# First experts of a two-layer transformer block: the neighbouring chunks' steps spread over a chunk's sixteen steps

## The chip, the cores and the metric

The kernel runs on one core of one Trainium2 chip. The metric is the device time of one execution in microseconds. Five engines work in parallel, each with its own instruction list: PE (TensorE, matmuls), DVE (VectorE), ACT (ScalarE), POOL (GpSimd) and SP (SyncE, which here issues all DMAs). They meet only through semaphores.

## What is computed

The input is 4 sequences of 1024 tokens with 128 features, fp32. Two layers follow each other, each attention and then a mixture of experts, with a layer norm after each half:

```python
x = _layernorm(x + _L0_attn_ref(x, Wqkv, Wout))        # 16 heads, causal, scores clipped
x = _layernorm(x + _L0_ffn_ref(x, Wg, W1, W2, W3))     # 8 experts, top 2, silu(x W1) * (x W2), then W3
x = _layernorm(x + _L1_attn_ref(x, w_qkv, w_out, b))   # 16 heads, full, rotary turn of q and k
x = _layernorm(x + _L1_ffn_ref(x, ...))                # 4 experts, top 2, gelu
```

Both expert layers compute all experts for all tokens and weigh them by gates, which are zero for the experts not chosen. The change lies in the second line, the first experts.

## The kernel before

Tokens go through the first experts in eight chunks of 512, features on the partitions. A chunk has sixteen steps (`SPC`), one for each tile of 128 hidden features, two steps for each of the eight experts. In a step n of chunk c:

- PE (`pe_chunk`) first runs what `pe_beside` has for the step, then the six hidden matmuls of step n + 3 (three for W1, three for W2, since each fp32 operand is split into an upper and a lower part), then the three matmuls of the product with W3.
- ACT (`act_chunk`) takes silu of the first hidden bank and copies the upper part of the previous step's product (`act_upper`), then runs `act_beside` for step n - 2.
- DVE (`dve_chunk`) multiplies the two hidden halves (L1447), subtracts to get the lower part of the step before (L1436), runs `dve_beside` for step n - 2, and in even steps weighs one expert's output by its gates (`dve_weigh`, L1427). Weighing 0 writes `y_sb`, the others write a part that POOL adds to it.
- POOL (`pool_experts0`) has one fixed list for a chunk: seven adds of weighed outputs (`pool_add`), the `pow` of both layer norms, and small pieces for the neighbours.

ACT and DVE are two steps late against PE (`LATE`); in the last steps of a chunk they reach into the next one's loop.

The "beside" steps belong to the neighbouring chunks. The front is chunk c + 1, which is still being prepared: output projection of the attention (`o_proj`), residual and statistics, normalisation (`norm`), turn into features by tokens (`x_turn`), router matmuls (`router`), the best two (`dve_top2`), the gates' weights (`weigh`), their turn (`g_turn`), from where SP stores and broadcasts them. The back is chunk c - 1, whose experts are done: turn of its output (`y_turn`), residual and statistics, normalisation into `x_out` (`norm2`), its turn (`x2_turn`), and the next layer's queries (`q`), keys (`k`) and values (`v`). Queries and keys get their rotary turn on DVE (L1370, L1371), are summed on POOL (`pool_rot`), copied by ACT, and their lower parts come from POOL (`pool_qk_lower`). `plan[0]` (L993) says in which of the sixteen steps each of these happens; all engines read the same table. Chunk 0 has no back, chunk 7 has no front, and after chunk 7 its own back steps run alone, between them the first score pairs of the next attention (`BESIDE_BACK`, L131).

Waits that matter here: `x_turn` on PE waits for DVE's normalisation; ACT at `norm2` copies `x_out` and at `x_turn` copies the turned tile twice, in program order; the router's matmuls wait for both of these copies; `x2_turn` waits for `norm2` and for `gate_pre`, the last instruction of the top two, as they share a PSUM bank; `v` waits for the keys' rotation; weighing 0 waits for `y_turn` of the chunk before. The reciprocals of the softmax sums (`dve_rcp`, L1378) run at beside-step 7, written as a number.

Of the kernel before, what the change touches and what calls it, by code (L numbers as in the profile page):

```python
# [15 lines left out]
B, T, D, H = 4, 1024, 128, 16  # L16
# [108 lines left out]
class Full:  # L125
# [2 lines left out]
    HEADS = (1, 3, 0, 2)  # L128
    TURN_0, TURN_1 = 10, 2
    FIRST = PAIRS - 2 * PAIRS_STEP  # L130
    BESIDE_BACK = {1: (0,), 2: (1,), 4: (2, 3), 7: (4,), 8: (5, 6), 9: (7,)}  # L131

    def __init__(self, sem):
        self.n = 1
# [72 lines left out]
def build_program(nc, d, out):  # L207
    with ExitStack() as ctx:
# [537 lines left out]
        def first_pairs(L):  # L746

            return range(1 + max(m for ms in L.BESIDE_BACK.values() for m in ms), L.FIRST)

        def pe_pair_beside_back(pe, L, n):  # L750

            for m in L.BESIDE_BACK.get(n, ()):
                if m == 0:
# [237 lines left out]
            pass  # L991

        plan = [Beside(), Beside()]  # L993
        for pl, steps in ((plan[0], (2, 4, 6, 7, 8, 9, 1, 1, 3, 4, None, 5, 8, 10)),
                          (plan[1], (5, 7, None, None, None, None, 1, 1, 3, 6, 8, 11, 13, None))):
            (pl.y_turn, pl.norm2, pl.x2_turn, pl.q, pl.k, pl.v,
             pl.o_turn, pl.o_proj, pl.norm, pl.x_turn, pl.hidden, pl.router, pl.weigh, pl.g_turn) = steps
# [517 lines left out]
        def pool_rstd(pool, pc, wait, sig, k, val):  # L1515
            pool.wait_ge(wait, val)
            pool.sem_inc(apart_pool, 1)
            pc.link(nc.gpsimd.tensor_scalar(rstd[:, k, :], mv[:, k, :, 1], EPS, None, ALU.add))
            nc.gpsimd.tensor_tensor(rstd[:, k, :], rstd[:, k, :], mhalf[:, :], ALU.pow).then_inc(sig, 1)
# [45 lines left out]
        def pool_experts0(pool, st):  # L1565
# [3 lines left out]
            for c in range(2 * B + 1):  # L1569
# [9 lines left out]
                    pool_fill_values(pool, layers[1])  # L1579
                if c > 0:  # L1580
                    pool_rstd(pool, pc, st.stats2, st.rstd2, 1, c)
                if front:
                    pool_x_lower(pool, st, c + 1)
                if c < 2 * B:
                    pool_add(pool, st, c, 1, 0)
                if front:
                    pool_gate_exp0(pool, st, c + 1)
                if c < 2 * B:
                    pool_add(pool, st, c, 2, 0)
                if c > 0:  # L1590
                    for a in range(2):
                        pool_rot(pool, st, c - 1, a)
                if c < 2 * B:
                    pool_add(pool, st, c, 3, 0)
                if c > 0:
                    for a in range(2):
                        pool_qk_lower(pool, st, c - 1, a)
                if c < 2 * B:
                    pool_add(pool, st, c, 4, 0)
                    pool_add(pool, st, c, 5, 0)  # L1600

        def pool_experts1(pool, st):
            pc = Chain(pool, st.pool_chain)
# [248 lines left out]
```

## Time and profile before

| | us |
|---|---|
| median of 3 runs | 1602.66 (1599.79 to 1603.99) |
| profiled execution | 1611.3 |
| its span, first to last instruction | 1609.5 |
| of it, the first experts (chunks 0 to 7) | about 317 to 681 |
| PE busy in the span | 1471.5 (91%) |
| DVE busy | 1400.4 (87%) |
| ACT busy | 1202.9 (75%) |
| POOL busy | 307.5 (19%) |
| mean granted TensorE clock | 0.952 of full |

The times in the profile are those of one execution. "Idle before" is the time that an engine stood still before an instruction, with the instruction that released it behind the arrow. Matmuls are pipelined, so starts are safer to read than durations.

### The profile page before, as it was taken

The page shows a single profiled execution, that of the slowest core. Times are in us where ns is not written, and L with a number is a line of the kernel's source. Part 1 is how long each engine was busy: PE and PEld are TensorE (multiplying, and loading weights), DVE is VectorE, ACT ScalarE, POOL GpSimd, SP SyncE. Part 2 cuts the span into 40 slices and gives each one's busy share as a digit, 9 for nine tenths or more (in the row PEclk, how much of TensorE's full clock was granted, in tenths as well). Part 3 has the DMA queues.
Part 4 walks back from the last instruction along what each step waited for, and adds up shares of the span by engine and source line. Part 5 has one row for each costly group of instructions (what it writes and reads, how often), then busy time and mean ns, then how long its engine had stood idle before and what let it go on. Part 6 is the DMA issues. An engine that isn't in the chain of part 4 may idle for free.

```text
span 1609.5 us, 32282 instructions
## 1 busy us (share of the span) xinstructions
PE 1471.5 (91%) x11200; PEld 797.1 (50%) x11200; DVE 1400.4 (87%) x2394; ACT 1202.9 (75%) x1897; POOL 307.5 (19%) x325
## 2 busy tenths in 40 slices
PE   7989898689999999969999999999999998999996
PEld 4333333377777777623333333333333334777775
DVE  5899999878888988887999999999999973788886
ACT  4999999644445454417999999999999986777775
POOL 0000000234455454420000000000000001234333
PEclk9899999799999998966999999999999997999999
DMA  6636432131224431111111111111111110211211
GB/s 203 203 106 182 120 102 86 49 107 40 96 93 127 128 108 66 66 41 51 46 37 37 46 45 38 42 37 36 37 36 36 37 32 28 69 56 63 75 56 40
DMA packets 71026, 116.76 MB, mean 73 GB/s; under 512 B 23808, under 2 KB 33920, under 8 KB 70272
## 3 DMA queue, kind: packets, MB, share of 16 engines
q1 hardware_dynamic: 70912, 115.21, 23.5%
q8 instruction: 75, 1.23, 0.3%
q14 instruction: 39, 0.32, 0.1%
HBM read 73.49 MB, written 41.16 MB: 71 GB/s over the span
## 4 chain that ended last, share of the span: by engine, by line
PE 61%; DVE 15%; ACT 10%; issue 10%; POOL 1%; DMA 1%; DVEq 0%; ACTq 0%; SPq 0%; POOLq 0%
PE full_o L718 14%; PE hid_pair L1031 12%; PE max_pair L689 11%; ACT cprobs L491 7%; PE bank L1134 7%; DVE negmax_h L808 5%; PE score L703 4%; PE causal_o L463 3%; PE triple L447 2%; PE bank L1066 2%; ACT o_sb L779 1%; DVE st L1284 1%; PE hid_pair L952 1%; PE bank L1094 1%; DVE hid_lo L1458 1%
## 5 line engine op out<-in xcount | busy, mean ns | idle before, releaser
L771 ACT ACTIVATE probs<-score 128x512 f32<-128x512 f32 x1024 | 546.6, 596 | 89.5 <-PE score L703 69.5
L808 DVE TENSOR_REDUCE negmax_h<-max_pair 128x2 f32<-128x1024 f32 x512 | 588.6, 1216 | 24.9 <-PE max_pair L689 24.8
L718 PE MATMUL full_o<-probs,v_st 128*32 128x256 f32 x4096 | 337.9, 403 | 17.7 <-ACT o_sb L779 17.7
L703 PE MATMUL score<-q_st,k_st 32*128 32x512 f32 x1024 | 319.9, 510 | 2.6 <-ACT probs L771 2.6
L689 PE MATMUL max_pair<-k_st,q_st 32*128 32x512 f32 x1024 | 264.7, 515 | 12.2 <-DVE negmax_h L808 10.8
L491 ACT ACTIVATE cprobs<-triple 128x1536 f32<-128x1536 f32 x192 | 258.4, 1713 | 5.2 <-PE triple L447 5.2
L689 PEld LDWEIGHTS max_pair<-k_st,q_st 32*128 32x128 f32 x1024 | 97.8, 188 | 236.7 <-DVE negmax_h L808 179.9
L1240 ACT ACTIVATE act_s<-hid_pair 128x512 f32<-128x512 f32 x128 | 76.7, 599 | 149.5 <-PE hid_pair L1031 149.5
L1031 PE MATMUL hid_pair<-x_hi,w_hi 128*128 128x512 f32 x384 | 171.3, 446 | 1.8 <-DVE x_lo L1401 1.0
L521 DVE TENSOR_SCALAR cprobs<-cprobs 128x1536 f32<-128x1536 f32 (+6 forms) x272 | 160.7, 618 | 2.9 <-ACT cprobs L491 2.9
L463 PE MATMUL causal_o<-cprobs,v_st 128*32 128x512 f32 (+3 forms) x1536 | 156.2, 502 | 2.2 <-DVE cprobs L521 2.2
L718 PEld LDWEIGHTS full_o<-probs,v_st 128*32 128x32 f32 x4096 | 83.3, 109 | 150.0 <-issue 94.5
L703 PEld LDWEIGHTS score<-q_st,k_st 32*128 32x128 f32 x1024 | 141.6, 187 | 28.8 <-ACT probs L771 19.5
L1031 PE MATMUL hid_pair<-x_lo,w_hi 128*128 128x512 f32 x384 | 154.6, 403 | 0.0
L1031 PE MATMUL hid_pair<-x_hi,w_lo 128*128 128x512 f32 x384 | 154.3, 402 | 0.0
L447 PE MATMUL triple<-q_st,k_st 32*128 32x512 f32 (+3 forms) x768 | 101.5, 429 | 28.7 <-ACT cprobs L491 26.0
L447 PEld LDWEIGHTS triple<-q_st,k_st 32*128 32x128 f32 x768 | 47.6, 186 | 135.5 <-ACT cprobs L491 127.1
L1248 ACT ACTIVATE hid_hi<-hid_pair,be 128x512 fp32r<-128x512 f32 x128 | 89.0, 695 | 24.9 <-PE hid_pair L1031 17.9
L1134 PE MATMUL bank<-hid_hi,w_hi 128*128 128x512 f32 x256 | 101.9, 398 | 1.4 <-DVE qk_lo L1436 1.3
L1134 PE MATMUL bank<-hid_hi,w_lo 128*128 128x512 f32 x256 | 101.4, 396 | 0.0
L568 POOL COPY v_st<-v_all 128x256 f32<-128x256 f32 x32 | 12.7, 400 | 434.6 <-PE causal_o L463 246.3
L520 DVE SCALAR_TENSOR_TENSOR cprobs<-cprobs,bound 128x256 f32<-128x256 f32 (+4 forms) x160 | 92.3, 577 | 3.9 <-ACT cprobs L491 2.5
(157 smaller groups left out, 2001.8 us busy)
## 6 DMA issues: line engine op xcount, KB each, us to landing
gate_all<-gate_scr SPq DMA_DIRECT2D x48, 512.0 KB, 4.3
o_scr<-o_sb SPq DMA_DIRECT2D x64, 256.0 KB, 2.1
k_st<-k_scr SPq DMA_DIRECT2D x64, 128.0 KB, 2.8
q_st<-q_scr SPq DMA_DIRECT2D x128, 64.0 KB, 2.5
k_st<-k_scr SPq DMA_DIRECT2D x64, 96.0 KB
q_st<-q_scr SPq DMA_DIRECT2D x64, 96.0 KB
q_scr<-qk_hi SPq DMA_DIRECT2D x18, 256.0 KB, 4.6
k_scr<-qk_hi SPq DMA_DIRECT2D x18, 256.0 KB, 4.5
```

The costliest lines, as they stand in the source:

```text
L447: last = nc.tensor.matmul(triple[n % 2][:, bk, off:off + w], k_st[p][rows, kt * P:(kt + 1) * P], q_st[p][rows, q0:q0 + w], start=True, sto ...
L463: last = nc.tensor.matmul(causal_o[qc][SLOT * j:SLOT * (j + 1), c0:c0 + w], v_st[p][:, kt, j, :], cprobs[at % CP][:, bk, off:off + w], sta ...
L491: nc.scalar.activation(cprobs[n % CP][:, :, :], triple[n % 2][:, :, :], ACT.Exp, scale=SCALE).then_inc(L.exp_done, 1)
L520: nc.vector.scalar_tensor_tensor(edge, edge, float(np.exp(-CLIP)), limit, ALU.max, ALU.min)
L521: ins = nc.vector.tensor_scalar(plain, plain, float(np.exp(-CLIP)), float(np.exp(CLIP)), ALU.max, ALU.min)
L689: last = nc.tensor.matmul(ring[slot][:, k, :], q_st[p][rows, qt * P:(qt + 1) * P], k_st[p][rows, half * CH:(half + 1) * CH], start=True, s ...
L703: nc.tensor.matmul(sbank[L.score_bank(e)][:, :], k_st[p][rows, kt * P:(kt + 1) * P], q_st[p][rows, q0:q0 + w], start=True, stop=True, tile ...
L718: last = nc.tensor.matmul(full_o[SLOT * j:SLOT * (j + 1), cols], v_st[p][:, kt, j, :], probs[s % NP][:, j, cols], start=(kt == 0 and part ...
L771: nc.scalar.activation(probs[s % NP][:, L.HEADS[j], :], sbank[L.score_bank(e)][:, :], ACT.Exp, scale=SCALE).then_inc(L.exp_done, 1)
L808: nc.vector.tensor_reduce(negmax_h[:, qt // TPC, half, heads[0]:heads[1] + 1:2, qt % TPC], ring[slot][:, :, :], AXX, ALU.max, negate=True) ...
L1031: last = nc.tensor.matmul(hbank[2 * k + n % h_banks[layer]], w[:, slice_of(n)], x[:, :], start=(a == 0), stop=(a == 2))
L1134: last = nc.tensor.matmul(y_bank[e % 2], w, x, start=(f == 0 and a == 0), stop=(f == per - 1 and a == 2))
```

## The change

The steps of the table for the first experts are moved: `y_turn` 2 to 3, `norm2` 4 to 6, `x2_turn` 6 to 8, `q` 7 to 9, `k` 8 to 11, `v` 9 to 12, `norm` 3 to 4, `x_turn` 4 to 6, `router` 5 to 7, `weigh` 8 to 10, `g_turn` 10 to 13. The output projection stays at 1. The pairs beside the last back steps are renumbered with them. POOL's list is reordered: each add comes one place earlier, the two rotation sums are separated by an add, and the two lower parts of q and k go to the end of the list.

```diff
-    BESIDE_BACK = {1: (0,), 2: (1,), 4: (2, 3), 7: (4,), 8: (5, 6), 9: (7,)}
+    BESIDE_BACK = {2: (0,), 3: (1,), 6: (2, 3), 9: (4,), 11: (5, 6), 12: (7,)}
...
-        for pl, steps in ((plan[0], (2, 4, 6, 7, 8, 9, 1, 1, 3, 4, None, 5, 8, 10)),
+        for pl, steps in ((plan[0], (3, 6, 8, 9, 11, 12, 1, 1, 4, 6, None, 7, 10, 13)),
                           (plan[1], (5, 7, None, None, None, None, 1, 1, 3, 6, 8, 11, 13, None))):
             (pl.y_turn, pl.norm2, pl.x2_turn, pl.q, pl.k, pl.v,
              pl.o_turn, pl.o_proj, pl.norm, pl.x_turn, pl.hidden, pl.router, pl.weigh, pl.g_turn) = steps
...
                 if c > 0:
                     pool_rstd(pool, pc, st.stats2, st.rstd2, 1, c)
+                if c < 2 * B:
+                    pool_add(pool, st, c, 1, 0)
                 if front:
                     pool_x_lower(pool, st, c + 1)
                 if c < 2 * B:
-                    pool_add(pool, st, c, 1, 0)
+                    pool_add(pool, st, c, 2, 0)
                 if front:
                     pool_gate_exp0(pool, st, c + 1)
                 if c < 2 * B:
-                    pool_add(pool, st, c, 2, 0)
+                    pool_add(pool, st, c, 3, 0)
                 if c > 0:
-                    for a in range(2):
-                        pool_rot(pool, st, c - 1, a)
+                    pool_rot(pool, st, c - 1, 0)
                 if c < 2 * B:
-                    pool_add(pool, st, c, 3, 0)
+                    pool_add(pool, st, c, 4, 0)
+                if c > 0:
+                    pool_rot(pool, st, c - 1, 1)
+                if c < 2 * B:
+                    pool_add(pool, st, c, 5, 0)
                 if c > 0:
                     for a in range(2):
                         pool_qk_lower(pool, st, c - 1, a)
-                if c < 2 * B:
-                    pool_add(pool, st, c, 4, 0)
-                    pool_add(pool, st, c, 5, 0)
```

## Rows read from the trace of the kernel before

**Rows 1.** Table by stretches, chunks from step 1 to step 1; busy, clock.
```profile
core 0: us, PE busy (x) PEld busy (x) DVE busy (x) ACT busy (x) POOL busy (x), PEclk, DMA share, GB/s
366.30:412.20 45.90, 42.97 (x193) 33.58 (x192) 40.73 (x93) 22.39 (x41) 23.00 (x18) 0.96 0.26 88
412.20:459.10 46.90, 43.26 (x194) 33.72 (x193) 40.85 (x93) 22.49 (x42) 22.96 (x18) 0.96 0.28 97
...
597.50:646.50 49.00, 46.13 (x194) 36.05 (x193) 40.72 (x93) 22.44 (x42) 21.28 (x17) 0.90 0.19 70
```

**Rows 2.** Waits in 366 to 646 us: waiting, releaser, total us, times, longest.
```profile
ACT x_tm L1190 <- DVE x_out L1292: 19.3, 6, 3.2
```

**Rows 3.** Timeline of PE: start, us, line, operation, [idle before <-releaser].
```profile
412.23 1.05 PE L1082 MATMUL bank<-w_o,ot 128*128 128x128 f32 x8
...
422.38 0.66 PE L946 MATMUL bank<-ident,xs 128*128 128x128 f32 x4 [2.43 <-DVE xs L1292]
...
426.34 1.03 PE L1102 MATMUL bank<-wg,xt 128*128 128x8 f32 x8 [1.21 <-ACT x_hi L1210]
...
433.51 1.88 PE L1066 MATMUL bank<-xt,w_qkv 128*128 128x512 f32 x4
...
448.65 0.40 PE L1031 MATMUL hid_pair<-x_hi,w_hi 128*128 128x512 f32 x1
...
450.73 0.40 PE L1031 MATMUL hid_pair<-x_hi,w_hi 128*128 128x512 f32 x1
...
476.99 0.63 PE L946 MATMUL bank<-ident,x_out 128*128 128x128 f32 x4 [0.62 <-DVE lead L1303]
```

**Rows 4.** Timeline of DVE in the same chunk, 412 to 443 us.
```profile
412.37 0.69 DVE L1447 TENSOR_TENSOR hid<-hid_pair,act_s 128x512 f32<-128x512 f32 x1
...
414.22 0.68 DVE L1384 TENSOR_TENSOR res<-x_tm,bank 128x512 f32<-128x512 f32 x1
...
416.25 0.66 DVE L1447 TENSOR_TENSOR o_sb<-hid_pair,act_s 128x512 f32<-128x512 f32 x1
...
421.22 1.11 DVE L1292 TENSOR_SCALAR xs<-res,mv,rstd 128x128 f32<-128x128 f32 x4
...
423.45 1.11 DVE L1292 TENSOR_SCALAR x_out<-res,mv,rstd 128x128 f32<-128x128 f32 x4
...
426.71 0.69 DVE L1447 TENSOR_TENSOR hid<-hid_pair,act_s 128x512 f32<-128x512 f32 x1 [1.56 <-ACT act_s L1240]
...
429.76 0.17 DVE L1303 TENSOR_TENSOR lead<-mx 128x4 f32<-128x4 f32 x1
...
436.64 0.54 DVE L553 RECIPROCAL s_rcp<-s_raw 128x64 f32<-128x64 f32 x1
...
440.44 0.16 DVE L1325 TENSOR_SCALAR p<-p 128x4 f32<-128x4 f32 x1
...
442.57 0.69 DVE L1427 TENSOR_TENSOR o_sb<-bank,gate_all 128x512 f32<-128x512 f32 x1
```

**Rows 5.** Timeline of ACT, its copies before the router of that chunk.
```profile
424.59 0.63 ACT L1190 ACTIVATE x_tm<-x_out 128x512 f32<-128x512 f32 x1 [3.22 <-DVE x_out L1292]
...
425.61 0.59 ACT L1210 ACTIVATE x_hi<-bank 128x512 fp32r<-128x512 f32 x1
```

**Rows 6.** Timelines of POOL and DVE where their instructions overlap.
```profile
420.04 1.04 POOL L1519 TENSOR_TENSOR rstd<-rstd,mhalf 128x4 f32<-128x4 f32 x1
...
420.62 0.68 DVE L1436 TENSOR_TENSOR qk_hi<-o_sb,hid_hi 128x512 fp32r<-128x512 f32 x1
...
451.06 1.28 POOL L1562 TENSOR_TENSOR y_sb<-y_sb,o_sb 128x512 f32<-128x512 f32 x1 [1.23 <-DVE o_sb L1427]
...
451.50 1.40 DVE L1436 TENSOR_TENSOR qk_lo<-o_sb,hid_hi 128x512 fp32r<-128x512 f32 x1
```

**Rows 7.** Table by stretches, columns as in rows 1, inside the sixth chunk.
```profile
614.00:618.00 4.00, 4.00 (x11) 3.02 (x11) 2.17 (x17) 1.12 (x2) 1.86 (x2) 0.50 0.00 0
```

**Rows 8.** Timelines of DVE and PE in chunk 0.
```profile
333.06 0.69 DVE L1427 TENSOR_TENSOR y_sb<-bank,gate_all 128x512 f32<-128x512 f32 x1 [4.25 <-DMA gate_all<-gate_scr]
...
336.03 0.99 PE L946 MATMUL bank<-ident,xs 128*128 128x128 f32 x4 [4.81 <-DVE xs L1292]
```

## The prediction

> **What bounds the kernel now.** I first cut the span by chunk. The change touches only the first experts, from about 317 to 681 us. In the table by stretches [rows 1] a chunk with both neighbours takes 45.7 to 46.9 us (three at 45.7 to 45.9, two at 46.8 and 46.9) and the sixth takes 49.0. PE is busy 43 of these 46 us, DVE 41, ACT 22, POOL 23. So two engines are near the limit, and the question is which one sets the pace at which step. The PE timeline [rows 3] answers it. A plain step takes 2.08 us (448.65 to 450.73), and PE has no idle time except at the neighbours' steps: 2.43 us before the turn of `xs` at step 4, 1.21 us before the router's matmuls at step 5, and in every other chunk 0.4 to 0.62 us before the turn of `x_out` at step 6. The DVE timeline [rows 4] shows why. DVE runs two steps late (`LATE`), and loop steps 3 to 6 carry two sets of statistics and two normalisations on top of its product (0.60), subtraction (0.60) and, in even steps, weighing (0.60). It is back to back from 412.37 to 425.1. Then ACT, which has waited for DVE's `x_out` (19.3 us in six chunks, [rows 2]), copies three tiles and lets the router go [rows 5]. So from PE's step 1 to the turn of `x_out` a chunk runs at DVE's pace, and from there to the next step 1 at PE's.
>
> The stage also loses time to the clock. After such waits the granted clock lies at 0.50, the 1.2 GHz level, for a few us [rows 7]. The three odd chunks average 45.8 us, so the excess of the others is 1.1, 1.0 and 3.2, together 5.3 us. I put that down to the clock.
>
> **Spreading the steps: the DVE part.** Nothing is added or removed. Every instruction has the same size, so only waits can change. I lay one chunk out, with t = 0 at PE's step 1 (412.4 before). Prices are read from start to start in [rows 4]: statistics 2.03 (414.22 to 416.25), a normalisation 1.02, reciprocal 0.54. DVE runs beside-step n in its loop step n + 2.
> - Loop step 3 (statistics of the front) is unchanged and ends at 3.9.
> - Step 4 now holds only product, subtraction and weighing 0. That weighing overwrites `y_sb` and must wait for the turn of `y_sb`, now PE's step 3, which is over at 0.89 + 2 x 2.07 + 0.44 = 5.5. It would have started at 5.1, so 0.4 is lost. End 6.1.
> - Step 5 (statistics of the back): 1.2 + 2.03, end 9.4. Step 6: 1.2, front normalised at 11.6, weighing 1 to 12.2. PE's turn of `xs`, now step 6, can't come before 12.0: this 2.43 us wait goes, leaving some 0.7 us in small waits of steps 5 and 6 for DVE's products.
> - Step 7 is plain. But POOL's `add` 1 now starts as soon as weighing 1 ends, and the subtraction meets it: beside an add a subtraction takes 1.40 instead of 0.68 [rows 6]. Plain 1.2 plus 0.8, end 14.2.
> - Step 8: 1.2 + 1.02, `x_out` is ready at 16.4. ACT again has the copy of `x_out` in front of the two copies for the router, because `norm2` and `x_turn` share step 6 as they shared step 4. From the end of `x_out` to the end of the last copy it took 1.75 [rows 4, 5], so the router starts at 18.2.
>
> Before, the router started at 426.34 - 412.39 = 13.95, at step 5. Two plain steps later is 18.1. So the router gains nothing. The two steps of air that PE gets (4.14) are two steps of work for DVE too: 1.2 + 1.2 + 0.6 for weighing 1, plus the 0.4 and the 0.8, make 4.2. PE reaches the router at 14.9 and waits about 3.2 us there instead of 2.43 + 1.21 at two places.
>
> - Step 9 carries the top two of the router and, since `dve_rcp` stays at the written 7 while `router` moves to 7, the reciprocal in front of them. From `x_out` to the end of `lead` it took 429.93 - 424.5 = 5.4 [rows 4], now 5.4 + 0.54, so 22.35. PE's turn of `x_out` waits for it (`gate_pre`): PE is there at 21.1 and waits 1.2 us. Before it was released at 17.6, and plus 4.14 that is 21.7. **Cost 0.6 us a chunk.** The reciprocal stood before in the step of the queries (at 436.64, [rows 4]), where DVE had idle time.
>
> **The later half.** Queries, keys and values go from 7, 8, 9 to 9, 11, 12. PE's `v` matmuls wait for the keys' rotation one DVE step ahead, as before, but the router's weights now lie in the DVE step in front of it. From the start of DVE's step 12: 1.2, weights 1.25 to 2.13 (2.13 beside POOL, from 440.44 to 442.57, [rows 4]; without the wait inside them some 0.9 less), weighing 0.6; then 1.2, 0.75 for meeting `add` 4, rotation 1.2. That is 6.2 to 7.1, against PE's 2 x 2.07 + 1.73 = 5.9 (matmuls of 433.51, [rows 3]; their four records span 1.88, and the next matmul starts after 1.73). **Cost 0.3 to 1.2 us, taken 0.35**, since `add` 3 and the first rotation sum should be done by then.
>
> POOL's list is put in the order in which its inputs now come, so nothing in it waits behind a later one. After `add` 5 it has two subtractions and the division in a row, about 6 us with DVE's subtractions between them; `add` 6 then ends about when weighing 7 wants it. DVE's slack there is over 1 us, cost 0 (bound 0.5). SP: gate rows leave three steps later (13), but are wanted at DVE's step 4 of the next chunk, seven PE steps (14 us) on, against one store and a load of 4.3 us: hidden, and so is the later store of q and k. If that cover failed, weighing 0 would stall as in chunk 0 (4.25 us, [rows 8]). The list `BESIDE_BACK` only renumbers the same order on PE and DVE: 0.
>
> **The ends.** In chunk 0 weighing 0 waits for its gates until 333.06 [rows 8]. PE stood at the turn of `xs` until 336.03. Now it goes on at step 4 as soon as DVE has its product, at 333.06 + 1.2 = 334.3, where the matmuls of that step started at 336.7: **2.4 us gained**, once (1.7 if only the idle time shrinks, 3.4 if the clock holds). In the last chunk POOL's late subtractions meet DVE's last ones, which PE waits for: 0 to 2 us, taken 0.5.
>
> **A rule against the rows.** POOL's `pow` for the back now runs beside the front's normalisation. Before, a subtraction beside the same `pow` took its usual 0.68 (at 420.62, the `pow` at 420.04, [rows 6]), so I charge nothing. The Trainium skill ("GPSIMD Engine Reference", Specifications) says that GpSimd shares its SBUF interfaces with VectorE, with contention for instructions with two SBUF inputs or in a 2-port mode. By that rule the normalisation could be held as well; it agrees with the 1.40 us beside an add, not with the 0.68 beside a `pow`.
>
> **The sum.** Six chunks at 0.6 + 0.35 = +5.7. Chunk 0: -2.4. Tail: +0.5. The clock: PE still stands idle for about 3 us and then 1.2 us in every chunk, so it will still fall. Part of the slow time lies where PE waits anyway. Between 0 and 1.7 us a chunk I take 0.7 (most odd chunks showed 0, the even ones 1): 4.2 in place of 5.3, -1.1. Net +2.7 us. The profiled execution's span of 1609.5 (1611.3 with what lies around it) would become 1612.2. It lay 0.5% above the median of the runs, 1602.66, which becomes **1605.4**.
>
> **Rivals.**
> 1. *Slower by the clock.* The sixth chunk stayed slow for about 10 us (its middle is in [rows 7]) and took 3.2 us more [rows 1]. The wait in front of it was 2.76 us, the longest of the six; mine is 3.2 us and a second one follows two matmul groups later. If every chunk falls like that, the clock costs 6 x 3.2 = 19.2 instead of 4.2: 1620. Against: chunk 0 waited 4.81 us and was slow only once. It decides from a wait of about 2.8 us. 0.20.
> 2. *Faster.* `add` 1 doesn't meet the subtraction and the turn of `y_sb` doesn't hold weighing 0 (-1.2 a chunk, -7.2), and the shorter waits leave the clock alone (-4.2): 1594. For: this is what spreading would give if DVE had air. Against: 1.40 us subtractions stand in almost every quiet step. 0.18.
> 3. *Nothing.* Both engines carry the same work, losses and chunk 0's gain cancel: 1602.7. 0.10.
> 4. *The shared interface.* The normalisation waits for the `pow`, 1 us a chunk: 1611. It is the rule named above. 0.05, since the row speaks against it.
> My forecast, 1600 to 1611 by the bounds above: 0.47.
>
> A measurement tells about 0.3% from no change: 1597.9 and 1607.5. Faster: 0.14 of rival 2 and 0.02 of mine, 0.16. Slower: rivals 1 and 4, and 0.13 of mine, 0.38. Same: 0.46. The range 1595 to 1617 leaves out parts of rivals 1 and 2.
>
> **What would show it.** Right: no PE wait at the turn of `xs` (step 6); one of 2.5 to 3.5 us before the router's matmuls, 0.8 to 1.5 before the turn of `x_out`, up to 0.8 before `v`; chunks of 46.5 to 47.5 us; a subtraction of about 1.4 us right after weighing 1. Wrong: chunks under 45.5; a router wait under 1.5 us; or clock spells of 10 us in most chunks.

## The result and the profile after

| | before | after | ratio, 95% interval |
|---|---|---|---|
| first comparison, 6 runs each | 1605.2 (1599.8 to 1607.3) | 1618.0 (1611.8 to 1621.8) | 1.0080 (1.0050 to 1.0110) |
| second comparison, `after_again`, 31 runs before and 10 after | 1606.8 (1602.9 to 1614.3) | 1613.9 (1612.1 to 1622.9) | 1.0032 (1.0012 to 1.0052) |
| profiled executions | 1611.3 | 1615.2 | |

Times are in us: the median, and the lowest and highest run. The ratio is taken over the runs and isn't the quotient of the two medians (that would be 1.0044 in the second comparison). The change made the kernel slower, by 0.3 to 0.8%, where the forecast said 0.2%. 1618 lies 1 us outside the forecast range. That range was counted from 1602.66, the median of three runs of before; with six runs it is 1605.2, and 2.5 of the 12.6 us between forecast and result come from there.

The two profiled executions differ by only 3.9 us. That is less than the change cost, since around the start of the next attention, which the change doesn't touch, the clock was at its 1.2 GHz level for 51 us before and for 31 us after, and from the first score to the end the trace of after is 9.4 us shorter. The stage is better read at its end, the first score matmul of the next attention. These are the PE timelines of before, after, and the second trace of after, in that order:

```profile
723.94 1.21 PE L703 MATMUL score<-q_st,k_st 32*128 32x512 f32 x3
```
```profile
737.19 1.20 PE L703 MATMUL score<-q_st,k_st 32*128 32x512 f32 x3
```
```profile
731.55 1.21 PE L703 MATMUL score<-q_st,k_st 32*128 32x512 f32 x3
```

From step 1 of chunk 0 (323.49, 323.88 and 321.55) that is 400.5 us before, and 413.3 and 410.0 after: 12.9 and 9.6 us more. The table by chunks of after (step 1 to step 1, columns as in rows 1) answers [rows 1]:

```profile
366.96:415.87 48.91, 44.75 (x194) 34.62 (x192) 40.65 (x93) 22.41 (x41) 23.08 (x18) 0.93 0.18 55
415.87:463.70 47.83, 43.70 (x193) 33.50 (x192) 40.07 (x92) 22.40 (x41) 23.07 (x18) 0.96 0.26 92
463.70:511.52 47.82, 43.66 (x194) 33.58 (x193) 40.04 (x92) 22.41 (x42) 23.05 (x18) 0.96 0.26 90
```

The chunks behind them take 47.82 and 47.84. PE and DVE do the same work as before and both have more idle time. PE's waits in the second of these chunks, against [rows 3] (its other waits are the ones at 426.29 and 451.86):

```profile
415.87 1.05 PE L1082 MATMUL bank<-w_o,ot 128*128 128x128 f32 x8
...
426.29 0.47 PE L1031 MATMUL hid_pair<-x_hi,w_hi 128*128 128x512 f32 x1 [0.60 <-DVE o_sb L1447]
...
434.47 1.03 PE L1102 MATMUL bank<-wg,xt 128*128 128x8 f32 x8 [3.04 <-ACT x_hi L1210]
...
439.01 0.68 PE L946 MATMUL bank<-ident,x_out 128*128 128x128 f32 x4
...
451.86 1.16 PE L1072 MATMUL bank<-w_qkv,xt 128*128 128x128 f32 x8 [0.41 <-DVE rot L1371]
```

The wait at the turn of `xs` is gone, the router starts 18.60 us after step 1, and the turn of `x_out` has no wait in this trace. DVE, POOL and ACT ahead of that router, against [rows 4 to 6]:

```profile
421.65 0.69 DVE L1427 TENSOR_TENSOR y_sb<-bank,gate_all 128x512 f32<-128x512 f32 x1 [0.70 <-PE bank L1053]
...
426.65 1.11 DVE L1292 TENSOR_SCALAR xs<-res,mv,rstd 128x128 f32<-128x128 f32 x4
...
428.88 1.39 DVE L1436 TENSOR_TENSOR qk_lo<-o_sb,hid_hi 128x512 fp32r<-128x512 f32 x1
...
431.58 1.10 DVE L1292 TENSOR_SCALAR x_out<-res,mv,rstd 128x128 f32<-128x128 f32 x4
...
438.46 0.17 DVE L1303 TENSOR_TENSOR lead<-mx 128x4 f32<-128x4 f32 x1
```
```profile
426.07 1.61 POOL L1519 TENSOR_TENSOR rstd<-rstd,mhalf 128x4 f32<-128x4 f32 x1
...
428.44 1.28 POOL L1562 TENSOR_TENSOR y_sb<-y_sb,o_sb 128x512 f32<-128x512 f32 x1 [0.76 <-DVE o_sb L1427]
```
```profile
432.72 0.63 ACT L1190 ACTIVATE x_tm<-x_out 128x512 f32<-128x512 f32 x1 [3.10 <-DVE x_out L1292]
```

So the layout of the first half stood, to 0.3 us. What the sum got wrong lies behind it and at the two ends.

### The profile page after: what moved, and what is told of

Its sections match the earlier page's. It is cut to its first block, busy times and chain, and to the rows that moved or that the text cites. A ratio compares the mean times of both kernels' runs of the same rounds, so it can differ in the third digit from the quotient of the medians.

```text
span 1613.4 us, 32282 instructions
## 1 busy us (share of the span) xinstructions
PE 1469.0 (91%) x11200; PEld 795.2 (49%) x11200; DVE 1398.7 (87%) x2394; ACT 1202.4 (75%) x1897; POOL 307.4 (19%) x325
## 4 chain that ended last, share of the span: by engine, by line
PE 54%; DVE 20%; issue 12%; ACT 11%; POOL 1%; DMA 1%; DVEq 0%; ACTq 0%; SPq 0%; POOLq 0%
PE full_o L718 13%; PE max_pair L689 10%; PE hid_pair L1031 10%; ACT cprobs L491 7%; DVE negmax_h L808 6%; PE bank L1134 5%; PE score L703 4%; PE causal_o L463 3%; PE triple L447 2%; DVE qk_lo L1436 1%; PE bank L1066 1%; DVE st L1284 1%; ACT o_sb L779 1%; DVE qk_hi L1436 1%; DVE hid L1447 1%
## 5 line engine op out<-in xcount | busy, mean ns | idle before, releaser
L718 PE MATMUL full_o<-probs,v_st 128*32 128x256 f32 x4096 | 331.2, 396 | 17.7 <-ACT o_sb L779 17.7
L689 PE MATMUL max_pair<-k_st,q_st 32*128 32x512 f32 x1024 | 262.0, 510 | 11.7 <-DVE negmax_h L808 10.2
L568 POOL COPY v_st<-v_all 128x256 f32<-128x256 f32 x32 | 12.6, 398 | 435.0 <-PE causal_o L463 246.3
```

The lines of the kernel that those rows point to most:

```text
L689: last = nc.tensor.matmul(ring[slot][:, k, :], q_st[p][rows, qt * P:(qt + 1) * P], k_st[p][rows, half * CH:(half + 1) * CH], start=True, s ...
L718: last = nc.tensor.matmul(full_o[SLOT * j:SLOT * (j + 1), cols], v_st[p][:, kt, j, :], probs[s % NP][:, j, cols], start=(kt == 0 and part ...
```

## The experiments

Chunk lengths below are from step 1 to step 1 in the traces, for chunks 1 to 5. Ratios are against the kernel before on the same chip. A "spell" is a stretch at the 1.2 GHz level; it is 3.4 us long unless another figure stands there. The "drain" is what follows the last chunk. Where an edit moves steps of the back, the list `BESIDE_BACK` is renumbered with it, which isn't shown.

### The changed kernel again

> The changed kernel once more. Theory 1 (DVE's chain sets the chunk, so its length repeats, and the clock's slow spells fall where they fall): chunks 2 to 6 at 47.8 us again, router wait 3.0 and turn of x_out without a wait again; chunk 1 at 48.9 only if it has a slow spell of 7 us again, else 47.8. The 2.3 us that the drain lost in the first profile come back or not with the slow spell there. Theory 2 (the extra 1.1 us of chunk 1 and the drain's 2.3 us belong to the order of the steps): both repeat to 0.2 us, whatever the clock does.

Chunks 47.89, 47.93, 47.84, 47.83, 47.75. The router's wait was 3.04 to 3.07. Chunk 1 had a 3.4 us spell in place of the 6.8 us one of the first trace, and was 1.0 us shorter. The first spell of the drain was 10.2 us long in place of 17.1, and from its turn of y to the first score the drain took 40.0 us (691.56 to 731.55; before 40.0), in place of 42.2. So theory 1: 1.0 + 2.3 us of the first trace belong to where the clock fell that time. The lasting loss is 9.6 us.

### The reciprocal behind the top two

```diff
-                if n == (pl.o_turn - 1 if front == 0 else (7, 10)[layer]):
+                if n == (pl.o_turn - 1 if front == 0 else (9, 10)[layer]):
```

> The changed kernel with the reciprocal of the softmax sums back in the beside-step of the queries (9) instead of in front of the router's best two (7); nothing else. Theory 1 (the reciprocal lies on the path to the turn of x_out, as the prediction charged with 0.6 us a chunk): the end of the best two comes 0.5 us earlier, a chunk takes 47.3 instead of 47.8 us, the kernel is about 3 us faster than the changed one. Theory 2 (between the router and the turn of x_out the profile of the changed kernel shows PE at the 1.2 GHz level and arriving 0.4 us after the best two are ready, so the slow clock is what is last there): chunk 47.7 to 47.8 us, under 1 us in all.

1614.5, ratio 1.0048 (1.0033 to 1.0064). Chunks 48.96, 47.81, 47.83, 47.82, 47.80: nothing gained. In the changed kernel PE is at half speed just behind the router and reaches the turn of `x_out` 0.4 us after `lead` is done (439.01 against 438.46 + 0.17), so an earlier `lead` helps nobody while the spell is there. `lead` did come earlier: 22.12 us after step 1 in place of 22.59. The line of this run, which began that chunk at 414.75:

```profile
436.87 0.17 DVE L1303 TENSOR_TENSOR lead<-mx 128x4 f32<-128x4 f32 x1
```

### The turn of y back at step 2

```diff
-plan[0], (3, 6, 8, ...
+plan[0], (2, 6, 8, ...
```

> The changed kernel with the turn of y_sb back at step 2 (it was 2 before the change, 3 after), so that DVE's first weighing of a chunk does not wait 0.70 us for it. Theory 1 (from step 1 to the router a chunk runs at DVE's pace, and this wait is part of it): the 0.70 us wait of DVE is gone, the router's matmuls start 0.5 to 0.7 us earlier in the chunk, a chunk takes 47.2 us instead of 47.8, in all 3 to 4 us faster than the changed kernel. Theory 2 (PE's clock or POOL sets the pace and DVE's wait is hidden): chunk stays at 47.8 us.

1616.8, ratio 1.0067 (1.0044 to 1.0090). The router comes at 18.0 in place of 18.6, its wait is 2.70. So the hold of weighing 0, 0.4 in my layout, is worth 0.6. The chunks scatter with the spells: 46.92 and 46.73 in the two without one, 47.73 and 47.53 in two with one, 48.76 in one with 6.8 us. Without a spell that is some 0.5 under the 47.4 of the next run.

### PE kept busy ahead of the router

```diff
                     if layer == 0:
+                        if back is not None:
+                            for _ in range(12):
+                                nc.tensor.matmul(bank[3][:, :], w_hi[0][:, slice_of(0)], x_hi[1 - par][:, :], start=True, stop=True)
                         pe.wait_ge(st.xt_ready, front + 1)
```

The results of the added matmuls are not used.

> The changed kernel with twelve extra 128x512 matmuls (0.23 us each, 2.8 us in all, into a PSUM bank that is free there, their result unused) where PE stands idle 3.04 us before the router's matmuls, in chunks 1 to 6. Theory 1 (DVE's chain of steps sets the router's start, the slow clock after it costs little): the clock stays at the 2.4 GHz level, the router starts where it did, a chunk takes 47.4 us, in all 2 to 4 us faster than the changed kernel. Theory 2 (the fall to the 1.2 GHz level after the 3 us wait is what makes the change slower): a chunk takes 46.1 us, in all 10 us faster. If the matmuls themselves delay the router, a chunk is longer.

1615.7, ratio 1.0058 (1.0036 to 1.0080). The clock stayed at 1.00 from chunk 0 to the drain:

```profile
365.85:413.20 47.35, 44.99 (x206) 34.65 (x204) 40.56 (x93) 22.40 (x42) 23.07 (x18) 1.00 0.19 56
```

The router still starts at 18.61, its wait being filled, and now the wait that I had forecast at the turn of `x_out` is there:

```profile
388.59 0.63 PE L946 MATMUL bank<-ident,x_out 128*128 128x128 f32 x4 [0.92 <-DVE lead L1307]
```

Chunks 47.35 to 47.50. So the clock costs the changed kernel 0.5 us a chunk, and at full clock the chunk is 47.4. Theory 1: the rest is DVE's.

### The copy of x_out behind the router's copies

```diff
-                if layer == 0 and n == pl.norm2:
-                    act.wait_ge(st.norm2, back + 1)
-                    nc.scalar.activation(x_tm[:, bass.ds(back * TPC, TPC), :], x_out[:, :, :], ACT.Copy).then_inc(st.x_kept, 1)
...
+            if layer == 0 and back is not None and n == pl.norm2:
+                act.wait_ge(st.norm2, back + 1)
+                nc.scalar.activation(x_tm[:, bass.ds(back * TPC, TPC), :], x_out[:, :, :], ACT.Copy).then_inc(st.x_kept, 1)
```

The copy stands last in ACT's step in place of ahead of the others.

> The changed kernel with one block of ACT's list moved: the copy of x_out, which waits for DVE's second normalisation, comes behind the two copies of the turned tile that the router needs, instead of in front of them. Theory 1 (both share step 6, so the router waits for DVE's step 8 through ACT's order): the 3.04 us wait before the router shrinks to under 1 us; the best two come about 1 us earlier, since ACT's two copies no longer lie behind x_out; a wait of 1 to 3 us appears before the turn of x_out; a chunk takes 46.3 to 46.8 us instead of 47.8, in all 6 to 9 us faster than the changed kernel. Theory 2 (DVE's total work per chunk is the bound and the order of waits does not matter): chunk stays within 0.3 us of 47.8.

1624.6, ratio 1.0121 (1.0094 to 1.0148): a clear miss. The router's wait did go (t = 15.4, PE no longer waits there). The whole of it came back, with more, two matmul groups later:

```profile
487.01 1.09 PE L946 MATMUL bank<-ident,x_out 128*128 128x128 f32 x4 [3.99 <-DVE lead L1303]
```

`lead` stands behind `x_out` in DVE's list, so letting the router go earlier moved it by 0.4 us only (22.2 after step 1, against 22.6). The longer single wait was followed by a spell in which PE had nothing left to wait for, and the chunks took 48.4 to 49.9.

### The normalisation of the back one step later

```diff
-plan[0], (3, 6, 8, 9, 11, 12, ...
+plan[0], (3, 7, 9, 10, 11, 12, ...
```

> The changed kernel with the back's second normalisation one step behind the turn of xs (7 instead of 6), so that ACT's step 8 has no copy of x_out in front of the router's copies, and the turn of x_out two steps behind the router (9 instead of 8), queries at 10. Theory 1 (two waits set the middle of a chunk: the router behind x_out through ACT's order, and the turn of x_out behind the best two, one step after the router): both waits shrink to under 1 us together, the best two end at about 20.8 us of the chunk instead of 22.6, PE starts its queries at about 23.5; a chunk takes 43.5 to 44.5 us instead of 47.8, in all 20 to 26 us faster than the changed kernel and 8 to 14 us faster than the kernel before. Theory 2 (DVE's total of 41 us with its waits for POOL is the bound of a chunk): a chunk stays above 46.5 us, since the time saved in the middle comes back in the later steps.

1615.1, ratio 1.0042 (1.0023 to 1.0060). With ACT's copy of `x_out` no longer in the router's step, the router's wait is gone (t = 15.4), but:

```profile
480.17 0.63 PE L946 MATMUL bank<-ident,x_out 128*128 128x128 f32 x4 [1.95 <-DVE lead L1303]
...
493.61 1.16 PE L1072 MATMUL bank<-w_qkv,xt 128*128 128x128 f32 x8 [1.35 <-DVE rot L1371]
```

Chunks 46.48 and 46.66 at full clock, 47.86 in the three with a spell. That is 0.7 to 0.9 better than 47.4, not the 3 to 4 that the vanished wait promised.

### The same in the kernel before

```diff
-plan[0], (2, 4, 6, 7, 8, 9, ...
+plan[0], (2, 5, 7, 8, 9, 10, ...
```

> The kernel before, with the same decoupling but no spreading: norm2 5 (one behind x_turn at 4), x2_turn 7 (two behind the router at 5), q 8, k 9, v 10; all else as before, POOL's list too. Theory 1 (the two couplings, not the crowding, cost the kernel before its time): the 1.21 us wait before the router and the 0.4 to 0.6 us before the turn of x_out are gone, the 2.4 us wait before the turn of xs stays; a chunk takes 43 to 44.5 us instead of 46.7, 12 to 20 us faster than the kernel before. Theory 2 (crowding is what costs): 45.5 us or more, since queries and weights now meet in one DVE step.

1608.9, ratio 1.0008 (0.9982 to 1.0034). Chunks 46.0 to 46.8, where 43 to 44.5 was the hope. The wait at the turn of `xs` grew to 2.9, and waits of 0.6 to 1.0 came in front of the values. Another miss of the same kind: the wait moved.

### POOL's add 1 ahead, in the kernel before

```diff
+                if c < 2 * B:
+                    pool_add(pool, st, c, 1, 0)
                 if front:
                     pool_x_lower(pool, st, c + 1)
-                if c < 2 * B:
-                    pool_add(pool, st, c, 1, 0)
```

> The kernel before with only one piece of the new POOL list: the first add comes in front of the lower part of x instead of behind it. Theory 1 (the earlier add meets a subtraction of DVE on POOL's path and costs 0.7 us wherever DVE is behind; in the old steps DVE stands idle right after it): 0 us, chunks at 45.7 to 46.9 as before. Rival (the new POOL list itself costs or gains): chunks move by 0.5 us or more.

1606.6, ratio 0.9976 (0.9959 to 0.9994). Chunks 46.0 to 46.8. The odd chunks are 0.2 to 0.4 longer, the total is not: the earlier add costs nothing that the time shows. The rest of POOL's new list was not tried by itself.

### Add 1 small

```diff
+            n_col = 8 if layer == 0 and e == 1 else 512
-            nc.gpsimd.tensor_tensor(y_sb[:, :], y_sb[:, :], y_part[layer][:, :],
+            nc.gpsimd.tensor_tensor(y_sb[:, 0:n_col], y_sb[:, 0:n_col], y_part[layer][:, 0:n_col],
```

> The changed kernel, but in the first experts POOL's add 1 covers 8 of 512 columns (part of the first weighed sum is left out). Only the meeting of that add with DVE's subtraction in step 7 goes. Theory 1 (the 1.40 us subtraction lies on DVE's path to x_out): that subtraction 0.68, x_out and the router 0.7 us earlier in the chunk (t = 17.7), chunks 47.1 in place of 47.8. Theory 2 (some other wait is next, as with the earlier steps that were moved): subtraction 0.68, router 0.7 earlier, but the chunk stays within 0.2 of 47.8, as a longer wait before the keys or the values takes it back.

1611.1, ratio 1.0034 (1.0014 to 1.0054). The router comes at 17.90, 0.7 earlier, and the chunk is 0.7 shorter, with a spell (47.1) and without (46.7):

```profile
364.36:411.04 46.68, 42.31 (x194) 32.39 (x193) 39.87 (x93) 22.42 (x42) 22.03 (x18) 1.00 0.19 57
411.04:458.14 47.10, 43.63 (x194) 33.73 (x193) 39.42 (x92) 22.42 (x42) 21.98 (x18) 0.96 0.29 92
```

One subtraction that meets one add costs the chunk its whole 0.7 us. Theory 1.

### All seven adds small, without and with the fill

```diff
+            n_col = 8 if layer == 0 else 512
```

> The changed kernel with all seven adds of the first experts cut to 8 of 512 columns (most of the weighed sum is left out). Theory 1 (DVE is the bound, and what POOL's adds take from it is part of that): every subtraction 0.68, DVE busy 36 to 37 us a chunk in place of 41, chunks 44 to 45, the router wait under 1.5 us. Theory 2 (the order of the steps is what costs, POOL's adds only fill waits of DVE): DVE's busy time falls the same but chunks stay over 46.5 with waits of 3 us before the router.

1608.4, ratio 0.9996 (0.9968 to 1.0024). Each theory is half right. DVE's busy time fell to 37 us, the router's wait only to 2.35, and the chunk did not get shorter:

```profile
363.64:411.66 48.02, 44.97 (x194) 35.01 (x193) 36.96 (x92) 22.40 (x42) 14.50 (x18) 0.93 0.18 58
```

The reason is in the clock's column: 0.93, where the changed kernel has 0.96. Chunks 1 to 5 now had 6.8 us of spell each; the sixth had none. This is one execution of ten: they took 1597.1 us at a mean clock of 0.965 to 1616.9 us at 0.949, so others had less of it. The same with the twelve matmuls of the fill:

> The changed kernel with the seven adds cut to 8 columns (part of the weighed sum is left out) and, in chunks 1 to 6, twelve matmuls whose results are unused in front of PE's wait before the router. With the adds cut alone, chunks stayed at 48.0 us: DVE was freer, but the granted clock fell to the 1.2 GHz level for 6.8 us a chunk in place of 3.4. Theory 1 (DVE was the bound and the clock took its gain back): with the fill the clock stays up, chunks 45.5 to 46.3, 1.2 us or more below the filled kernel with whole adds (47.36). Theory 2 (the adds cost nothing; the order of the steps and PE's own work hold the chunk at 47.4): 47.2 to 47.5 with the clock up.

1605.4, ratio 0.9978 (0.9956 to 1.0000):

```profile
364.06:409.98 45.92, 44.47 (x205) 34.76 (x204) 36.85 (x92) 22.41 (x41) 14.53 (x18) 1.00 0.20 60
```

At full clock the adds cost the changed kernel 1.4 us a chunk (47.35 against 45.92). Without the fill a chunk had 2.1 us of clock loss in that trace (48.02), where the changed kernel has 0.5, so that nothing was left to see.

### The kernel before, filled, and with small adds

```diff
                 if n == pl.x_turn:
+                    if layer == 0 and back is not None:
+                        pe.wait_ge(st.stats2, back + 1)
+                        for _ in range(10):
+                            nc.tensor.matmul(bank[3][:, :], w_hi[0][:, slice_of(0)], x_hi[1 - par][:, :], start=True, stop=True)
                     pe.wait_ge(st.norm, front + 1)
```

> The kernel before with ten matmuls whose results are unused in front of PE's wait for the normalisation (turn of xs), chunks 1 to 6. Theory 1 (a spell at 1.2 GHz costs what the difference of its chunks showed, the rest is DVE's pace): clock at full speed through chunks 1 to 6, every chunk at 45.7 to 45.9 us, 4 to 5 us less than before in all. Theory 2 (chunks of 46.8 and 49.0 us have another cause than the clock, or the fill delays the matmuls behind it by as much): alternation of 45.9 and 46.8 stays, no gain.

1610.9, ratio 1.0024 (1.0003 to 1.0045): no gain. The stage isn't longer in the trace (399.7 us, before 400.5), so the few us more are not explained. Chunks 45.86, 46.81, 45.93, 46.69, 46.72. The fill took away the spells of the first and third, and those two are no shorter than before. In the second and fourth the spell stayed and so did the 46.7 to 46.8. In the fifth it moved from 10 to 16 us after step 1, and the chunk became 1.0 us longer. The sixth lost its 10.2 us spell and is 2.8 us shorter (45.25 in place of 48.07, from turn of y to turn of y). The trace of before says why, once all chunks are looked at:

```profile
376.00:380.00 4.00, 3.45 (x12) 2.77 (x13) 3.32 (x9) 1.25 (x3) 0.00 (x0) 0.65 0.00 0
428.00:432.00 4.00, 4.00 (x14) 3.17 (x13) 3.38 (x19) 1.71 (x3) 2.44 (x3) 0.57 0.01 4
468.00:472.00 4.00, 2.90 (x10) 2.41 (x11) 3.88 (x12) 0.78 (x3) 0.00 (x0) 0.67 0.00 0
520.00:524.00 4.00, 4.00 (x14) 3.11 (x14) 3.21 (x19) 1.11 (x2) 3.00 (x3) 0.57 0.02 4
```

The odd chunks had their spells too, about 10 us after step 1, where PE still waits for DVE (it is busy for 2.9 to 3.5 of the 4 us). There the half speed costs nothing. In the even ones the spell lay 16 us after step 1, behind the router, where PE is back to back: 0.9 us each.

> The kernel before with the seven adds of the first experts cut to 8 of 512 columns (part of the weighed sum is left out). In the changed kernel the same cut, with the clock up, took a chunk from 47.36 to 45.92 us. Theory 1 (in the kernel before, the adds lie where DVE has air behind the router, so they cost nothing there, and the change moved them onto DVE's path): at full clock chunks stay at 45.5 to 45.9, the turn of x_out at t = 17.5 to 17.9. Theory 2 (the adds cost the same in both orders, and the 1.5 us that the change adds at full clock is not theirs): chunks 44.4 to 44.6 at full clock, so the changed order is 1.4 us longer with or without the adds.

1604.2, ratio 0.9979 (0.9960 to 0.9997):

```profile
366.84:412.05 45.21, 41.67 (x193) 32.44 (x192) 39.10 (x92) 22.41 (x41) 13.94 (x18) 1.00 0.28 91
```

> The same with ten matmuls whose results are unused in front of PE's wait for the normalisation, so that fewer slow spells blur the lengths. Theory 1: chunks without a spell 45.5 to 45.9. Theory 2: 44.4 to 44.6.

1602.2, ratio 0.9964 (0.9944 to 0.9984). Chunks 45.19, 45.20, 45.41, 45.20, 45.21. Neither theory: the adds cost the kernel before 0.65 us a chunk at full clock, about half of what they cost the changed one.

### A combination

```diff
-plan[0], (3, 6, 8, 9, 11, 12, 1, 1, 4, 6, None, 7, 10, 13)
+plan[0], (2, 7, 9, 10, 11, 12, 1, 1, 4, 6, None, 7, 9, 13)
-(7, 10)[layer]
+(12, 10)[layer]
```

> The steps y_turn 2, norm2 7, x2_turn 9, q 10, k 11, v 12, norm 4, x_turn 6, router 7, weigh 9, g_turn 13, the reciprocal at 12, POOL's list as in the changed kernel. It joins the experiments before. Theory 1: a chunk of 42.3 to 43.5 us, the clock at the 2.4 GHz level in most chunks, 12 to 20 us faster than the kernel before. Theory 2 (DVE's total is the bound): no better than the variant with norm2 at 7 alone.

**1600.0 (1595.1 to 1604.6), ratio 0.9937 (0.9905 to 0.9968)**: faster than both kernels, though by 8 us and not by the 12 to 20 of theory 1, whose chunk of 42.3 to 43.5 did not come either. Theory 2 is out as well: the variant with the later normalisation alone took 46.5 to 46.7. Chunks 46.27, 44.98, 44.94, 44.83, 45.77:

```profile
456.22:501.16 44.94, 41.97 (x193) 32.47 (x192) 40.66 (x93) 22.40 (x41) 22.09 (x18) 1.00 0.30 94
```

There is no spell between chunk 0 and the last. PE's idle time comes in small pieces (0.9, 1.4 and 0.6 us, none at the router). Then two variants, the weights at step 10 (first) and the values at step 13 (second):

```diff
-(2, 7, 9, 10, 11, 12, 1, 1, 4, 6, None, 7, 9, 13)
+(2, 7, 9, 10, 11, 12, 1, 1, 4, 6, None, 7, 10, 13)
+(2, 7, 9, 10, 11, 13, 1, 1, 4, 6, None, 7, 9, 13)
```

> The combined version with the router's weights back in step 10 in place of 9. Theory 1 (the weights lie in the DVE step in front of the rotations of the keys and hold the values' matmuls; in step 9 they fall where DVE has air): 0.8 to 1.5 us longer a chunk than the combined version (46 in place of 45), a wait of 1.5 to 2 us before the values. Theory 2 (the gain came from the earlier turn of y_out and the later normalisation, or from the clock that stayed up): chunks within 0.3 of 45.

1606.4, ratio 1.0002 (0.9987 to 1.0017). Chunks 46.1 to 46.3 from the second on, also without a spell: 1.3 us longer, with 1.57 us in front of the values. Theory 1 on the size; part of its cause is another. DVE's subtractions in one chunk, weights at 10 and then at 9 (columns: us, DVE busy with these 16 instructions, clock):

```profile
458.80:505.06 46.26, 17.86 (x16) 1.00 0.30 93
```
```profile
456.22:501.16 44.94, 15.74 (x16) 1.00 0.30 94
```

The same 16 subtractions take 2.1 us more, because the step's place decides which of them meets a POOL instruction: 31.8, 34.9 and 40.8 us after step 1 they take 1.40, 1.38 and 1.38 with the weights at 10, where with 9 none behind 25 us takes more than 1.12.

> The combined version with the values one step later (13 in place of 12), nothing else. Theory 1 (a wait in front of the values is only where DVE's lag shows; moved later, it shows elsewhere): chunks within 0.2 us of 44.9, the wait now elsewhere. Theory 2 (that wait is a loss by itself): 0.5 us less a chunk, 44.4.

1597.8, ratio 0.9950 (0.9935 to 0.9966). Chunks 46.22, 44.95, 45.03, 45.02, 45.76: the same. Theory 1.

## Why the prediction was wrong

The forecast was +2.7 us for the stage; its parts, against the second trace of after (up to the first score):

| | forecast | measured |
|---|---|---|
| chunk 0 | -2.4 | +0.1 |
| chunks 1 to 6 | +4.6 | +6.9 |
| chunk 7 and what follows | +0.5 | +2.5 |
| sum | +2.7 | +9.6 |

**What held.** The layout to the router: forecast 18.2 from DVE's first product, which starts 0.16 behind PE's step 1, so 18.4 from there; measured 18.6. "The router gains nothing" was right, as were the vanished wait at `xs`, the 3.2 us before the router (3.04), the 0.4 us of weighing 0 (in the trace 0.70 idle, worth 0.6 in the run with the old turn), the 1.39 us subtraction right behind weighing 1, and the 0.35 us before the values (0.41). One reading was a little off: the 1.75 us from `x_out` are those to the router's start (1.78); the last copy ends at 1.64. The shared interface (rival 4) is refuted: the normalisation beside the 1.61 us `pow` took its 1.11.

**The steady chunk at full clock.** The four kernels that separate it, as us after step 1 (before with fill, chunk 1; after with fill; the two with small adds):

| | router | turn of x_out | values | next step 1 |
|---|---|---|---|---|
| before | 14.14 | 17.86 | 27.99 | 45.86 |
| after | 18.61 | 22.74 | 35.52 | 47.35 |
| after, less the plain steps moved (4.14, 4.14, 6.21, 0) | +0.33 | +0.74 | +1.32 | +1.49 |
| before, small adds | 13.48 | 17.21 | 27.34 | 45.21 |
| after, small adds, filled | 18.13 | 22.04 | 34.23 | 45.92 |
| the same difference | +0.51 | +0.69 | +0.68 | +0.71 |

Without the adds, the new order costs 0.7 us, all of it by the turn of `x_out`: the 0.6 of my sum, at its place. I called the reciprocal its cause. Moving that alone brought `lead` 0.47 us forward, so it does stand on that path, but the chunk gained nothing at the clock of that kernel; at full clock it wasn't tried, so what it costs a chunk stays open. (The fill holds the router of the last kernel by 0.2 us. In the sixth chunk without fill, which has no spell, the router starts at 17.90, but the turn of `x_out` and the values at 22.03 and 34.22, as with fill.)

With the adds there are 0.8 us more. Ahead of the turn of `x_out` both orders lose 0.7 us to an add (14.14 against 13.48, 18.60 against 17.90), but not to the same one. In the old order it is the last add of the chunk before, which holds the first subtraction behind step 1; here with whole adds (step 1 at 367.10) and with small ones (366.84):

```profile
367.36 1.30 POOL L1567 TENSOR_TENSOR y_sb<-y_sb,o_sb 128x512 f32<-128x512 f32 x1 [2.63 <-DVE o_sb L1432]
367.85 1.35 DVE L1441 TENSOR_TENSOR qk_lo<-o_sb,hid_hi 128x512 fp32r<-128x512 f32 x1
```
```profile
367.60 0.68 DVE L1436 TENSOR_TENSOR qk_lo<-o_sb,hid_hi 128x512 fp32r<-128x512 f32 x1
```

In the new order that meeting is covered, since weighing 0 waits for the turn of y behind it (with add 1 alone made small the router comes as early as with all of them small), and it is add 1 that costs 0.7. The other 0.8 us come between the turn of `x_out` and the values (1.32 - 0.74 = 0.6, where small adds give none) and behind them (0.2). The 0.6 is one meeting, with add 4, in the filled kernel; the same subtraction with small adds below it:

```profile
398.28 1.28 POOL L1566 TENSOR_TENSOR y_sb<-y_sb,o_sb 128x512 f32<-128x512 f32 x1 [2.57 <-DVE o_sb L1431]
398.71 1.40 DVE L1440 TENSOR_TENSOR qk_hi<-o_sb,hid_hi 128x512 fp32r<-128x512 f32 x1
```
```profile
396.22 0.68 DVE L1440 TENSOR_TENSOR qk_hi<-o_sb,hid_hi 128x512 fp32r<-128x512 f32 x1
```

In the old order nothing is lost there (31.7 us from the router to the next step 1, with whole and with small adds).

My sum had this meeting, 0.75 for add 4, and what it assumed ("`add` 3 and the first rotation sum should be done by then") held: the weights took 1.2 us. The wait before the values came as forecast, 0.41 for 0.35. **The step that failed is what was booked for it**: I took the wait that PE shows there for the whole cost, and 0 (bound 0.5) for the steps behind. Measured are 0.6 and 0.2, so 0.8 us a chunk in place of 0.35. The same step failed at both ends, with more weight: chunk 0 behind the router was put at nothing (1.2 us), the last chunk at 0.5 (1.8 to 2.5); both are below. The subtractions of one chunk of before, after, before with small adds, and after with small adds:

```profile
459.06:504.99 45.93, 14.58 (x16) 0.96 0.28 88
```
```profile
511.52:559.34 47.82, 14.93 (x16) 0.96 0.35 106
```
```profile
366.84:412.05 45.21, 12.93 (x16) 1.00 0.28 91
```
```profile
364.06:409.98 45.92, 11.71 (x16) 1.00 0.20 60
```

Making the adds small shortens DVE's subtractions by 1.65 us a chunk before and by 3.2 after, and the chunk by 0.65 and 1.43. With whole adds the two sums are nearly the same, 14.6 and 14.9: the change hardly lengthened them, it laid the long ones elsewhere. Of the subtractions above 0.75 us in these chunks five of eight stand beside an add before, and three of seven after; the others meet POOL's other pieces. What the chunk pays for is one meeting with an add before (0.66) and two after (0.70 and 0.6), besides 0.1 behind the values that no single instruction shows.

**The clock.** I took the difference between odd and even chunks for "spell or no spell", so 5.3 us before. What the difference shows is where the spell lies. As a sum it is nearly right by luck: before's six chunks averaged 46.70 against 45.86 at full clock, 0.84 each or 5.0, of which the sixth (10 us of spell) has 3.1 (2.8 by the filled kernel). After has one spell in every chunk, behind the router, for 0.5 each or 3.0. So -2.0 in place of my -1.1, which hid part of what the layout missed. Together (6 x 1.49 - 2.0) that is the measured +6.9. Rival 1, a clock loss of 3.2 in each chunk, did not come: it rested on the wait's length, and 3.04 us waits were followed by 3.4 us spells and once by one of 6.8, while 2.76 was once followed by 10 us. Rival 2's second half, the clock left alone, came only in the filled versions of the changed kernel and in the combinations.

**Chunk 0.** The router came 1.1 us early against the old 16.70 and two steps (341.29, 19.74 after step 1, in the second trace). In the filled kernel, which has no spell in this chunk, it came at 17.79, so 3.0 early. I had named both ends (1.7 with the idle time alone, 3.4 if the clock holds) and taken the middle; the spell came right behind PE's wait again, as before, and the gain was that of the idle time (3.69 in place of 4.81; the gates also came 0.4 us later in that trace, 9.99 after step 1 against 9.57). Behind the router, where my working ended, the rest of the chunk took 23.2 us against 22.0 (26.11 less two steps); with small adds 22.05. So the adds took the other 1.2. The clock would not have saved the term: in the filled kernel the rest took 24.5 us, and the whole chunk 42.27 against 42.81 before, a gain of 0.5; with small adds and no spell it took 40.13.

**The last chunk.** From its turn of y, one step later in the new plan, to the first score it takes 75.8 us, and before 75.4: with 2.1 for the step, 2.5 more, against 0.5 (range 0 to 2). With small adds the two traces with 6.8 us of spell there give 73.0 for the old order and 71.9 for the new one (from its later step), 1.0 more. The filled kernels with whole adds, 76.0 and 76.3, give 1.8 in place of 2.5. So 1.0 us belongs to the order and 0.8 to 1.5 to the adds. The forecast had only the late subtractions in it.

All three misses, 2.3, 2.5 and 2.0, have POOL's adds in them, and to that extent the same reason: I charged in full only where I had laid DVE's path out instruction by instruction. What the 1.0 us of the order in the last chunk consists of stays open.

## What to carry to other kernels

When work is spread more evenly on the engine that sets the pace, count for every step which of its instructions will run beside another engine's on the same memory, and give each meeting its price; here up to 0.7 us each, nothing where that engine waits behind it anyway (the first one in the changed chunk), all of it where it doesn't (add 1). A wait that vanishes is a gain only if the engine behind it is done earlier: the change itself, the later normalisation and the new order of ACT's copies each removed a wait of 2 to 3 us and got 0.9 us a chunk for it at best. To split a loss between engines and clock, fill the wait with idle matmuls and shrink the suspected work, together; in the changed kernel either alone showed nothing or a third.

## What the runs showed of the hardware

**What an add of POOL catches.** Beside a 1.28 us add of two 512-column tiles, DVE's subtraction of two SBUF tiles takes 1.40 in place of 0.68. Products that read PSUM kept 0.69 beside such an add, and the normalisation kept 1.11 beside a `pow` (none met an add). A product of only 4 columns, both inputs in SBUF, is caught as well: 1.05 us in place of 0.16 in the combination with the weights at 10, beside a rotation sum of POOL:

```profile
441.39 1.05 DVE L1327 TENSOR_TENSOR p<-p 128x4 f32<-128x4 f32 x1
```
```profile
441.14 1.27 POOL L1524 TENSOR_TENSOR rot<-rot 128x512 f32<-128x512 f32 x1 [3.23 <-DVE rot L1371]
```

It ends when the sum that it meets does (442.44 and 442.41), so even a tiny operation can cost 0.9 us. The Trainium skill ("GPSIMD Engine Reference", Specifications) names instructions with two SBUF inputs as the ones in contention. The traces agree for these two and for the products that read PSUM and were not held. They don't for a subtraction beside a `pow`, which has two SBUF inputs and kept its 0.68.

**Where a spell costs.** A 3.4 us spell cost 0 where PE was waiting anyway, 0.5 in the changed chunk, where a 0.9 us wait covers part of it, and 0.9 to 1.0 behind the router of the kernel before. In chunk 0 of the changed kernel it cost 0.7 with whole adds (42.95 against 42.27) and 1.6 with small ones (41.70 against 40.13). One of 6.8 us cost 2.1 with small adds, one of 10.2 us 2.8 in the sixth chunk of before. In the trace with less work on DVE and the same on PE the spells were 6.8 us in place of 3.4, so a gain on another engine can be lost to TensorE's clock; that the lighter work brought the longer spells is not shown by one trace.
